# New hand-written stage orders for a four-batch software pipeline on one Trainium2 core

## The reference, cut to what matters

```
x = x + cross_attention_0(layernorm(x), ctx)     # 8 heads of 64, masked softmax over 64 keys
x = x + expert_ffn_0(layernorm(x))               # 16 experts of 64, top 4 by sigmoid score
x = x + cross_attention_1(layernorm(x), ctx)     # 4 heads, top 32 of 64 scores, FiLM on both sides of
                                                 # a convolution along the 512 tokens (done by Fourier
                                                 # transform), then layernorm, W1, gelu, W2, layernorm
x = x + expert_choice_ffn(x)                     # 8 experts, each takes its 512 best of all 4096 rows
```

## Time and profile before

| what | value |
|---|---|
| median of 3 runs | 1681.39 us (1681.15 to 1682.14) |
| the profiled execution's own time | 1687.38 us |
| its span, first to last instruction | 1685.6 us, mean granted TensorE clock 0.860 |
| PE busy | 1360.9 us (81%) |
| DVE busy | 935.8 us (56%) |
| ACT and POOL busy | 477.0 us (28%) and 330.9 us (20%) |

### The profile page before, as it was taken

The page is one execution under the profiler, slowest core; times in us unless marked ns, Lnnn a source line. Parts: engine busy times, 40 slices in busy tenths (PEclk is TensorE's granted clock), DMA queues, the critical chain, the costliest instruction groups (busy, mean ns, idle before and its releaser), DMA issues. The chain is left out here.

```text
span 1685.6 us, 17715 instructions
## 1 busy us (share of the span) xinstructions
PE 1360.9 (81%) x5358; PEld 828.3 (49%) x5358; DVE 935.8 (56%) x3450; ACT 477.0 (28%) x837; POOL 330.9 (20%) x600
## 2 busy tenths in 40 slices
PE   2685956699799889979979988997994641999997
PEld 2453534354554545545454554545452341567674
DVE  6656556755767475576666757557676338211111
ACT  2334221024216213321621422242041213231221
POOL 3132111011203201120320320112021121323322
PEclk9876877799699879969989997996996775899999
DMA  8002000200200030020002002003000014243511
...
DMA packets 44857, 72.56 MB, mean 43 GB/s; under 512 B 8085, under 2 KB 26648, under 8 KB 44634
## 3 DMA queue, kind: packets, MB, share of 16 engines
...
## 5 line engine op out<-in xcount | busy, mean ns | idle before, releaser
L595 POOL TENSOR_SCALAR ve<-mv 128x2 f32<-128x2 f32 x80 | 18.3, 229 | 836.8 <-DVE mv L850 836.6
L1336 PE MATMUL ps<-x,keys 128*128 128x512 f32 x256 | 142.4, 685 | 0.3 <-DVE hT L942 0.3
L1336 PE MATMUL ps<-zT_second,w 128*128 128x512 f32 x256 | 124.9, 627 | 2.7 <-ACT big L1301 1.4
L1490 PE MATMUL ps<-hT,values 128*128 128x512 f32 x256 | 119.1, 593 | 0.0
L1336 PE MATMUL ps<-w,big 128*128 128x256 f32 x512 | 113.6, 381 | 5.5 <-ACT big L1301 4.7
L1941 PE MATMUL experts_ps<-experts_yT,experts_fc 128*128 128x512 f32 x256 | 113.3, 601 | 1.3 <-ACT experts_yT L1864 1.3
L1953 PE MATMUL experts_ps<-experts_fc,experts_hT 128*128 128x256 f32 x512 | 112.1, 380 | 0.8 <-ACT experts_hT L1876 0.8
L1336 PEld LDWEIGHTS ps<-w,big 128*128 128x128 f32 x512 | 96.6, 190 | 27.4 <-ACT big L1301 9.6
L1953 PEld LDWEIGHTS experts_ps<-experts_fc,experts_hT 128*128 128x128 f32 x512 | 96.6, 190 | 14.7 <-ACT experts_hT L1876 1.6
L1839 DVE SCALAR_TENSOR_TENSOR experts_o<-experts_ps,experts_wh,experts_b2w 128x256 f32<-128x256 f32 x32 | 15.5, 484 | 140.2 <-PE experts_ps L1953 140.2
L1336 PE MATMUL ps<-vf,amT 65*128 65x512 f32 x128 | 81.2, 747 | 13.2 <-ACT amT L1183 12.3
...
## 6 DMA issues: line engine op xcount, KB each, us to landing
gT<-expert_gates SPq DMA_DIRECT2D x16, 1024.0 KB, 9.7
experts_fc<-in_fc1T SPq DMA_DIRECT2D x8, 1024.0 KB, 5.3
experts_fc<-in_fc2T SPq DMA_DIRECT2D x8, 1024.0 KB, 9.4
...
xT<-in_xT SPq DMA_DIRECT2D x8, 512.0 KB, 3.5
x<-in_x SPq DMA_DIRECT2D x8, 512.0 KB, 3.5
out_x<-x SPq DMA_DIRECT2D x8, 512.0 KB, 11.3
w<-in_W SPq DMA_DIRECT2D x2, 1024.0 KB, 8.5
```

What stands on the lines that cost most here:

```text
L595: nc.gpsimd.tensor_scalar(o, i, c, None, ALU.add).then_inc(*tick(*event))
L1336: last = nc.tensor.matmul(o, l, r_, start=start, stop=stop)
L1490: last = nc.tensor.matmul(bank("O2", k), S["values"][:, c, k * P:(k + 1) * P], hT[:, c % RING, :], start=(c == 0), stop=(c == HC - 1))
```

## The change

All five lists are replaced. No stage is added, removed or altered, no list gains or loses a stage, and the two functions that walk the lists stay as they are. The core of the diff is the list that is used six times:

```
 ORDER = [
-    (LAST, "film_in", 0), (LAST, "film", 0), (MID, "mlp", 0), (LAST, "film", 1), (LAST, "transform"), (MID, "mlp", 1), (LAST, "film_in", 1),
-    (MID, "text", 0), (LAST, "fold"), (MID, "text", 1), (MID, "relu", 0), (MID, "relu", 1), (MID, "mlp", 2), (LAST, "turn"),
...
-    (ATTEND, "soften", 3), (MID, "weigh"), (LAST, "gelu", 5), (MID, "text", 2), (ATTEND, "attend", 4), (LAST, "gelu", 6),
...
-    (MID, "pick", 2, 0), (MID, "pick", 2, 1), (ATTEND, "attend_out"), (MID, "pick", 2, 2), (ATTEND, "attend_sum"), (LAST, "ffn_out", 1),
-    (LAST, "ffn_add", 0), (ATTEND, "route"), (LAST, "norm_out", 0), (MID, "pick", 2, 3), (LAST, "scores", 0), (MID, "pick", 3, 0),
-    (MID, "pick", 3, 1), (ATTEND, "gates", 0), (LAST, "ffn_add", 1), (ATTEND, "gates", 1), (LAST, "norm_out", 1), (ATTEND, "gates", 2),
-    (ATTEND, "gates", 3), (LAST, "scores", 1), (MID, "picked", 0), (LAST, "route_experts"), (LAST, "table"), (LAST, "shift_scores"),
-    (MID, "pick", 3, 2), (ATTEND, "spread"), (MID, "pick", 3, 3), (MID, "picked", 1),
+    (LAST, "film_in", 0), (MID, "mlp", 0), (LAST, "film", 0), (MID, "mlp", 1), (LAST, "film_in", 1), (MID, "relu", 0), (LAST, "film", 1),
+    (LAST, "transform"), (MID, "relu", 1), (LAST, "fold"), (LAST, "turn"), (MID, "relu", 2), (MID, "mlp", 2), (MID, "mlp", 3),
+    (LAST, "product", 0), (MID, "relu", 3), (MID, "text", 0), (MID, "mlp", 4), (LAST, "product", 1), (LAST, "product", 2), (MID, "mlp", 5),
...
+    (LAST, "film_out", 2), (ATTEND, "keys", 1), (LAST, "film_out", 3), (MID, "text", 1), (ATTEND, "norm"), (LAST, "norm_ffn"),
...
+    (MID, "pick", 1, 2), (ATTEND, "soften", 3), (LAST, "gelu", 5), (ATTEND, "attend", 3), (MID, "pick", 1, 3), (ATTEND, "soften", 4),
+    (LAST, "gelu", 6), (LAST, "gelu", 7), (ATTEND, "attend", 4), (LAST, "ffn_out", 0), (ATTEND, "attend_out"), (MID, "pick", 2, 0),
+    (LAST, "ffn_add", 0), (MID, "pick", 2, 1), (MID, "pick", 2, 2), (LAST, "ffn_out", 1), (ATTEND, "route"), (LAST, "norm_out", 0),
+    (ATTEND, "attend_sum"), (MID, "pick", 2, 3), (MID, "pick", 3, 0), (LAST, "ffn_add", 1), (MID, "weigh"), (LAST, "norm_out", 1),
+    (ATTEND, "gates", 0), (LAST, "scores", 0), (MID, "pick", 3, 1), (ATTEND, "gates", 1), (ATTEND, "gates", 2), (ATTEND, "gates", 3),
+    (LAST, "scores", 1), (MID, "picked", 0), (MID, "text", 2), (LAST, "shift_scores"), (MID, "pick", 3, 2), (LAST, "route_experts"),
+    (ATTEND, "spread"), (MID, "pick", 3, 3), (LAST, "table"), (MID, "picked", 1),
 ]
```

More of the change, by code:

```diff
@@ L130 @@
+    (ATTEND, "attend_out"), (ATTEND, "attend_sum"), (ATTEND, "route"), (KERN, "powers", 2), (ATTEND, "gates", 0), (ATTEND, "gates", 1),
+    (ATTEND, "gates", 2), (KERN, "centre", 4), (ATTEND, "spread"), (ATTEND, "gates", 3), (KERN, "phases", 4), (KERN, "film_row"),
+    (KERN, "powers", 3), (KERN, "centre", 5),
 ]
 SECOND = [
-    (MID, "text", 0), (MID, "mlp", 0), (KERN, "phases", 5), (MID, "text", 1), (MID, "mlp", 1), (KERN, "powers", 4), (MID, "relu", 0),
-    (MID, "relu", 1), (MID, "relu", 2), (MID, "mlp", 2), (MID, "mlp", 3), (MID, "relu", 3), (MID, "mlp", 4), (MID, "mlp", 5),
@@ new lines @@
+    (MID, "pick", 2, 1), (KERN, "kernel", 1), (MID, "pick", 2, 2), (MID, "pick", 2, 3), (MID, "pick", 3, 0), (ATTEND, "attend", 4),
+    (KERN, "kernel", 2), (MID, "pick", 3, 1), (ATTEND, "attend_out"), (ATTEND, "attend_sum"), (KERN, "kernel", 3), (ATTEND, "route"),
+    (MID, "picked", 0), (MID, "pick", 3, 2), (ATTEND, "gates", 0), (MID, "pick", 3, 3), (ATTEND, "gates", 1), (KERN, "kernel", 4),
+    (ATTEND, "gates", 2), (ATTEND, "gates", 3), (KERN, "kernel", 5), (ATTEND, "spread"), (MID, "picked", 1), (MID, "text", 2),
@@ L179 @@
-    (MID, "pick", 1, 1), (MID, "stats_rows", 1), (LAST, "gelu", 6), (LAST, "gelu", 7), (MID, "text", 2), (MID, "pick", 1, 2),
-    (LAST, "ffn_out", 0), (MID, "pick", 1, 3), (MID, "pick", 2, 0), (MID, "pick", 2, 1), (LAST, "ffn_out", 1), (MID, "pick", 2, 2),
-    (MID, "pick", 2, 3), (LAST, "ffn_add", 0), (MID, "pick", 3, 0), (LAST, "norm_out", 0), (MID, "pick", 3, 1), (LAST, "scores", 0),
-    (LAST, "ffn_add", 1), (LAST, "norm_out", 1), (LAST, "scores", 1), (LAST, "route_experts"), (MID, "picked", 0), (LAST, "table"),
@@ L183 @@
-    (MID, "pick", 3, 2), (MID, "pick", 3, 3), (LAST, "shift_scores"), (MID, "picked", 1),
+    (MID, "mlp", 0), (LAST, "film_in", 0), (LAST, "film_in", 1), (MID, "relu", 0), (LAST, "film", 0), (MID, "mlp", 1), (MID, "relu", 1),
+    (LAST, "fold"), (MID, "relu", 2), (LAST, "turn"), (LAST, "film", 1), (LAST, "transform"), (MID, "relu", 3), (LAST, "product", 0),
+    (MID, "mlp", 2), (MID, "relu", 4), (LAST, "product", 1), (LAST, "product", 2), (MID, "relu", 5), (MID, "mlp", 3), (MID, "mlp", 4),
@@ L184 @@
+    (MID, "pick", 3, 0), (MID, "pick", 3, 1), (LAST, "ffn_out", 1), (LAST, "ffn_add", 0), (MID, "weigh"), (LAST, "norm_out", 0),
+    (LAST, "scores", 0), (LAST, "ffn_add", 1), (LAST, "norm_out", 1), (MID, "text", 2), (LAST, "scores", 1), (LAST, "route_experts"),
+    (MID, "pick", 3, 2), (MID, "picked", 0), (LAST, "shift_scores"), (LAST, "table"), (MID, "pick", 3, 3), (MID, "picked", 1),
 ]
 FINAL = [
-    (LAST, "film", 0), (LAST, "film_in", 0), (LAST, "film", 1), (LAST, "transform"), (LAST, "film_in", 1), (LAST, "fold"), (LAST, "turn"),
@@ L192 @@
-    (LAST, "ffn_out", 0), (LAST, "ffn_out", 1), (LAST, "norm_out", 0), (LAST, "ffn_add", 1), (LAST, "norm_out", 1), (LAST, "scores", 0),
-    (LAST, "scores", 1), (LAST, "route_experts"), (LAST, "table"), (LAST, "shift_scores"),
+    (LAST, "film", 0), (LAST, "film_in", 0), (LAST, "film_in", 1), (LAST, "fold"), (LAST, "hold"), (LAST, "film", 1), (LAST, "turn"),
+    (LAST, "transform"), (LAST, "product", 0), (LAST, "product", 1), (LAST, "back", 0), (LAST, "product", 2), (LAST, "product", 3),
+    (LAST, "unfold"), (LAST, "back", 1), (LAST, "turn_back"), (LAST, "film_out", 0), (LAST, "film_out", 1), (LAST, "film_out", 2),
@@ new lines @@
+    (LAST, "back", 2), (LAST, "film_out", 3), (LAST, "norm_ffn"), (LAST, "back", 3), (LAST, "ffn"), (LAST, "gelu", 0), (LAST, "ffn_add", 0),
+    (LAST, "gelu", 1), (LAST, "gelu", 2), (LAST, "gelu", 3), (LAST, "norm_out", 0), (LAST, "ffn_add", 1), (LAST, "norm_out", 1),
+    (LAST, "gelu", 4), (LAST, "gelu", 5), (LAST, "gelu", 6), (LAST, "gelu", 7), (LAST, "ffn_out", 0), (LAST, "ffn_out", 1),
+    (LAST, "scores", 0), (LAST, "scores", 1), (LAST, "route_experts"), (LAST, "shift_scores"), (LAST, "table"),
```

71 lines of the change are left out of this document (29 added, 42 removed).

## The result

| kernel | median us (range) | ratio to before, 95% |
|---|---|---|
| before | 1681.77 (1681.15 to 1682.55) | 1 |
| after | 1548.53 (1542.68 to 1551.76) | 0.9204 (0.9174 to 0.9233) |

The new lists take 133 us off, where 74 were forecast. The profiled execution of the changed kernel took 1542.68 us (the fastest of the four) with a span of 1540.9.

The account below looks back on a forecast made before the run. In each ORDER trip PE was taken to bound the first stretch and a DVE chain the second. ORDER 50, DRAIN 9, FIRST and SECOND 17, less FINAL 2, make 74 us off: 1607 us, range 1580 to 1650.

Parts of the forecast that it names:

- DRAIN: The trip after the ORDER trips: text 2 and mlp 1 leave, idle time falls; 9 us less, bounds 3 and 12.
- FINAL: Last trip: hold before film 1's copy on ACT waits for a store; costs 2 us, range 0 to 7.
- Stretch A: ORDER trip, end of transform to end of ffn_out 1, bound by PE: 106.7 us becomes 97.2, bounds 95 and 104.
- a sign of being wrong: The prediction is wrong if DVE waits for back 0 or for gT; no size was given for the wait.
- Stretch B: ORDER trip, end of ffn_out 1 to end of next transform: 36.9 us becomes 37.4, bounds 35 and 41.
- a chain through DVE is the bound: After ffn_out 1 in ORDER: adds, gates, last picks and picked 1 on DVE set the time, 23.9 us.
- the slow case: text 2 ahead of route_experts at the lower level, 7.3 us; result 16.5 us after ffn_out 1, shift_scores waits about 1.5.
- mlp 0 and mlp 1 stand before film 1: End of an ORDER trip: both stages delay film 1, which needs picked 1 anyway; 0 to 3 us more.
- The rival "better": text 2, mlp 0 and mlp 1 keep the clock up in more of stretch B; 1584 us, chance 0.16.
- The trips in sum: Six ORDER trips, 9.0 us less each: 54, taken as 50; bounds 8 lost and 78 won.
- FIRST and SECOND: The two starting trips: three DVE waits of 7.1 us go, 4 comes back; 17 us less, bounds 4 and 30.
- the term of 4: In FIRST, phases 3 now waits for the products of powers 1, which gives 4 us back.

Follow-up runs that it names:

- text2_back: The changed kernel with text 2 of the six ORDER trips back behind gelu 5, as before the change; 1563.99 us, ratio 0.9298.
- mlp_late: The changed kernel with mlp 0 of ORDER back behind film 0 and mlp 1 back behind transform; 1573.52 us, ratio 0.9325.
- picks_early: The changed kernel with six picks of ORDER earlier: 2,1 to 3,0 ahead of ffn_add 0, 3,1 and 3,2 ahead of ffn_add 1; 1555.53 us, ratio 0.9223.
- text2_late: The changed kernel with text 2 of ORDER moved from behind picked 0 to behind spread; 1567.44 us, ratio 0.9313.
- text2_thin: The changed kernel with each product of text 2 cut from 512 columns to 64 in all trips; 1535.03 us, ratio 0.9136.
- shift_mid: The changed kernel with pick 3,2 and shift_scores of ORDER ahead of picked 0, text 2 left in place; 1562.70 us, ratio 0.9288.
- mlps_ahead: The changed kernel with mlp 1 of ORDER ahead of film 0 too; 1555.65 us, ratio 0.9248.
- order_only: The kernel before with the new ORDER list alone; 1611.57 us, ratio 0.9579.
- powers_moved: The kernel before with one edit in SECOND: soften 2, attend 2, then powers 6 and 7 ahead of pick 0,3 and shift; 1674.25 us, ratio 0.9930.
- start_only: The kernel before with the new FIRST and SECOND lists alone; 1636.59 us, ratio 0.9732.
- drain_only: The kernel before with the new DRAIN list alone; 1670.95 us, ratio 0.9903.

## Why the prediction missed, step by step

The prediction lacked 59 us. By the kernels with one list each, SECOND and FIRST lacked 28 of them, the ORDER trips 21, DRAIN 7; the rest is FINAL, which cost nothing that shows, and what is left over. In the two traces the trips' share looks larger, 32 us, for the reason given with the result.

**Stretch A: right.** 97.2 us predicted with bounds of 95 and 104, 96.1 measured. text2_back gives 3.5 us for text 2 (3.65) and mlp_late 1.7 for mlp 1 (1.8). POOL's long wait is gone, PE's new waits are 1.1 us and less, the clock is 1.00. back 0 waits for nothing. relu 0 waits 1.1 us for gT, which the prediction named as a sign of being wrong; it is small, and what failed lies elsewhere.

**Stretch B: the first of two steps that failed.** "B becomes 37.4; bounds 35 and 41" stands against a mean of 33.0. The figure is 36.9 plus 0.5, and the text does not add it up from its terms. The path was wrong: "a chain through DVE is the bound", up to picked 1. In the trip of the earlier trace rows picked 1 ended at 741.24, and the transposes for film 1 came 3.7 us later, right behind mlp 0, with no wait:

```profile
744.94 0.56 PE L1538 MATMUL ps<-ident,am 128*64 128x128 f32 x2
```

picks_early shows the same by experiment: picked 1 comes 1 us earlier and B stays. The chain through DVE, POOL and ACT ends at `sct` and film 0's `amT`, and behind it B is PE's work at the level that it is given. Two terms were wrong with it. First, text 2 was priced ahead of route_experts with 3.65 to 7.3 us, and a wait of shift_scores as the consequence, with the result of route_experts 16.5 us behind ffn_out 1 in the slow case. It was there at 12.1 us: route_experts would have waited 3.43 us anyway (text2_late), and at the level that text 2 lifted it took 1.95 us instead of the 3.58 that I had put down for it. Second, "mlp 0 and mlp 1 stand before film 1, which needs picked 1 anyway: 0 to 3 us more": mlp_late has them in the old places and its B is 2.6 us longer, not shorter. The clock is in both, and I had B's mean of 0.63 and did not look at the level in the head by itself. From film 0's products to the end of B the kernel before takes 16.4 us (from 737.95) and a short trip of the changed kernel 11.1 (from 653.68), with mlp 1 in it besides; nearly all of B's gain is there.

**The rival "better" had the right stretch and half of the cause.** It said that text 2 and mlp 0 and 1 keep the clock up in more of B. The place of mlp 0 and 1 matters (mlp_late). text 2 does lift the level where it stands, which makes it free, and B is no shorter for it (text2_thin). "DVE's chain does not care", which the prediction held against this rival, is what picks_early refutes. Two sums of the prediction are uneven, and neither matters for the miss: the bound of 8 us lost leaves out the 4 us that the 78 won take off, and from 0.97 to 0.80 it is 17 us a trip, not 16.5.

A rule of the Trainium skill bears on what is left. In the changed kernel's trips of 31.6 us the head runs at 2.4 GHz from film 0 on, in the one of 37.4 most of it at 1.2, with the same instructions. The Trainium skill, TensorE: Matmul & The Clock Gate, Part 1, says that how many products run slow varies with one and the same kernel, because the monitor's watch is not aligned with the program. The trace agrees in what can be seen: six passes of one list, three lengths. That the alignment is the cause no run here shows. The mean of 33.0 is such a mixture, four trips near 31.6 and one each of 33.7 and 37.4, where I had only one number.

**What sets the level in the head stays open.** The hole of 3.4 us at `sct` is there in good and in slow trips. Splitting it (shift_mid), filling it (text2_late) and putting more behind it (mlps_ahead) each left a part of the head slow in most trips, but each moved other waits too. The twelve passes of this list in the changed kernel and in order_only show how regular it is. In the five of 31.6 or 31.7 us the level comes back 18.4 to 19.5 us behind ffn_out 1, ahead of film 0; in those of 32.2 and 33.7 at 21.0 and 21.2; in the five of 36.9 to 37.6 at 27.9 to 28.5. The fall before it comes 15.0 to 16.1 us behind ffn_out 1 in four of the first five (12.3 in the fifth), and 14.2 to 14.9 in the other seven. So a few tenths of a microsecond between the program and the fall go with a B that is 6 us longer. This is a regularity of twelve passes: no run shifted the one against the other. order_only has the same list as the changed kernel and four slow trips of six in place of one, which makes 6 x (35.5 - 33.0) = 15 us in B.

**The trips in sum.** 50 us predicted, 82.5 measured. Before, A and B together have a mean of 142.9 us, which bears out the deduction from 54 to 50. The other 33 us are A with 6 x 1.1 = 7 and B with 6 x 4.4 = 26. By the medians the list is worth 70.8 us (order_only), with more slow heads; which of the two is nearer to a usual execution of the changed kernel one profile does not tell.

**FIRST and SECOND: the second step that failed, and by the medians the larger.** 17 us predicted with bounds of 4 and 30, 45 measured. The 14.2 us of line 873 were sized right, as the trace of powers_moved shows. In FIRST the waits at line 873 fell from 11.3 to 6.5 us in the trace of start_only (the longest from 7.1 to 2.5), and 3.7 us came at phases 3 (line 771), as the term of 4 said; nothing was left of it. The term that failed is the one put at nothing: the other waits of SECOND, 26.3 us in four lines. I had priced the waits whose cause I could name and bounded the sum by "a quarter of all that idle time"; the new list takes more than half of the 64.5 us.

**DRAIN.** 9 us predicted with a bound of 12, 14.6 measured in the trace and 16.3 by drain_only, part of which is DRAIN's head. A went from 82.2 to 69.1 us: idle time fell by 4.4 (5.3 to 0.9) and busy time by 8.7, of which 5.45 were counted. Of the other 3.2 the clock gives some 1.6: an estimate from 82.2 us at 0.98 and 69.1 at 1.00. The rest stays open. The tail gave 1.5 more, which I had not priced.

**FINAL: within its bounds.** hold ahead of film 1's copy was priced at 2 us out of 0 to 7. ACT in FINAL:

```profile
1141.56 1.04 ACT L1288 COPY x<-x_kept 128x1024 f32<-128x1024 f32 x1 [2.94 <-DMA out_x<-x]
1144.05 0.37 ACT L1183 COPY amT<-ps 64x256 f32<-64x256 f32 x1 [1.44 <-PE ps L1538]
```

hold waits 2.94 us for the store, as said, and the second `amT` copy behind it then waits for PE and not for hold. From film 0 to the end of table FINAL is 0.7 us longer, and from transform to there it is the same (82.0 us in both), so hold itself cost nothing.
